# A graph network on one Trainium2 core: fourteen tails of the first layer run as a software pipeline between VectorE and ScalarE

## The chip, the core and the metric

The kernel runs on one core of a Trainium2 chip, as one program. The metric is the device time of one launch in microseconds (us), the median of several runs. All five engines take part: TensorE (PE in the profile, with its weight loads as PEld), VectorE (DVE), ScalarE (ACT), GpSimd (POOL) and SyncE (SP, whose queue issues DMAs).

## The reference, cut to what matters

Four graph layers in a row over 12,500 nodes with 64 features and 212,500 edges. Each layer normalizes `x`, clips it at zero, sums something over the edges into their target nodes and adds the result to `x`. The change lies between the first and the second:

```python
edge_index = jnp.stack([src, dst])
h = jnp.maximum(_layernorm(x, axis=-1), 0.0)
x = x + _L0_gnn_ref(h, L0_gnn_W, src, dst)              # sum of h[src] * W over the edges
h = jnp.maximum(_layernorm(x, axis=-1), 0.0)            # what the changed stage computes
x = x + _L1_gnn_ref(h, edge_index, ...)                 # two mean aggregations with dense layers
...
def _layernorm(x, axis=-1, eps=1e-05):
    m = jnp.mean(x, axis=axis, keepdims=True)
    v = jnp.var(x, axis=axis, keepdims=True)
    return (x - m) / jnp.sqrt(v + eps)
```

## The kernel before, in words

**Layout.** Nodes lie in 98 tiles of 128 (`T` = 98, one node per partition); seven tiles are a batch (`B7` = 7), so there are 14 batches (`NBAT`) of 128 x 448 numbers. `xs` holds x in float32. The sum over the edges is a matrix product with a table of edge counts: `cells` in DRAM holds for each pair of nodes how many edges join them, as bytes, SyncE loads it in chunks of 224 KB, VectorE and ScalarE turn the bytes into bfloat16 by turns (lines 616 and 1400), and TensorE multiplies (line 1650). The other operand is a table `tab` of h, split into three bfloat16 terms (high, middle, low) that add up to the float32 value.

**The first product** (layer 0, `p` = 0) runs beside other work of the kernel. Counts too large for a byte are made up for by a short list: GpSimd adds its sums to `extra` in DRAM, and what it holds is known only at the end of the product. So after the last tile's sums are read out (lines 652 and 653) and the last plain tail (`tail0`, line 755) is done, the loop `for m in range(NBAT): late0(m)` (line 810) runs the 14 late tails, one batch after the other. Nothing of the second product can start before its last table row is made.

**One late tail**, `late0(m)`, is 12 instructions of VectorE and one of ScalarE, in strict order. Line 761 adds the list's counts to `has`, line 762 the list's rows to `xs`. `norm` computes the sum over the features (line 631, to `mean7`), the centred rows (632, `cen`), their squares (633, `sq`) and the sum of the squares (634, `var7`); ScalarE takes the root (1394, `sd7`); VectorE inverts it (637, `rs7`), then scales and clips (638, `hrow`). `split` makes the table's three terms: the high term is a cast (642), the rest a subtraction (643), the middle term a cast (644), the low term a subtraction (645). Then ScalarE's queue issues the DMA of the batch's table rows to `trow` in DRAM (`keep_rows`, line 1403).

**What sets the order.** Each engine's order is that of the text. Every instruction of VectorE here goes through `link`, which raises the semaphore `s_prep` and makes the next instruction wait for it:

```python
def link(ins):
    steps[0] += 1
    ins.then_inc(s_prep, 1)
    dve.wait_ge(s_prep, steps[0])
    return steps[0]
```

On SyncE's queue `load_ext(0, m)` (line 1218) loads the list's rows of batch m into one of two buffers, 227.5 KB each; from the third on it waits until `late0(m - 2)` has read its buffer. After the last of them SyncE issues a load of 832 KB (line 1281) and the first nine chunks of `cells` for the second product, whose ring has nine places. GpSimd waits for all the rows of `trow` and then gathers from it (`list_get`, line 1080).

## Time and profile before

| | |
|---|---|
| median of 3 runs | 6922.79 us (6919.97 to 6924.64) |
| the profiled execution | 6921.18 us, of which the span from the first to the last instruction is 6919.3 us |
| DVE busy | 4606.4 us (67%) |
| ACT busy | 3720.1 us (54%) |
| PE busy | 5262.2 us (76%) |
| late tails (lines 761 to 645, 14 times) | from 2591.62 to 2694.47 us of the span |

The span counts from the first instruction. "Busy" is the time in which an engine has an instruction in hand; the durations of two neighbours on one engine can overlap. "Idle before" a group is the time its engine stood still just ahead of its instructions, with what ended it behind the arrow.

### The profile page before, as it was taken

Reading aid. Unit: us, or ns where it says so; the run is one execution under the profiler, and the core shown is the slowest. Engines: PE = TensorE matmul, PEld = TensorE weight load, DVE = VectorE, ACT = ScalarE, POOL = GpSimd, SP = SyncE. Lnnn points to the kernel's source line nnn. Section 1 sums busy time; section 2 is a strip of 40 time slices with the busy share of each in tenths; the row PEclk is TensorE's granted clock in tenths of the full one; section 3 lists DMA queues with packets and bytes.
Section 4 is the critical chain, followed back from the end, with each engine's and each line's share of the span. In section 5 each row is a group of like instructions: output and inputs, shape, how many; then the busy total and the mean of one; then the engine's idle time right before and its main releaser. Section 6 shows DMA issues by size and latency. Waiting matters only on the chain.

```text
span 6919.3 us, 127730 instructions
## 1 busy us (share of the span) xinstructions
PE 5262.2 (76%) x47666; PEld 4799.9 (69%) x47667; DVE 4606.4 (67%) x6014; ACT 3720.1 (54%) x2906; POOL 3433.8 (50%) x3412
## 2 busy tenths in 40 slices
PE   0057478888888753999999999855888888788886
PEld 0023267777777653999999999855777777677776
DVE  9757567777777658788877888733555555555554
ACT  0100167666666543788777777600555454454565
POOL 0457777777777750000000000077777777777730
PEclk9988789999999886999999999977999999999998
DMA  9999977666666545666666666533777677676785
GB/s 344 351 273 297 335 234 215 209 214 210 212 214 215 175 117 141 181 195 194 191 189 186 195 196 197 161 80 90 158 151 159 153 156 154 140 155 148 157 143 110
DMA packets 1628347, 1313.89 MB, mean 190 GB/s; under 512 B 911250, under 2 KB 1528211, under 8 KB 1627311
## 3 DMA queue, kind: packets, MB, share of 16 engines
q1 hardware_dynamic: 840725, 948.43, 46.1%
q10 hardware_dynamic: 674448, 299.80, 18.4%
q0 software_dynamic: 112592, 57.76, 5.1%
q8 instruction: 382, 6.26, 0.4%
q14 instruction: 200, 1.64, 0.1%
HBM read 833.34 MB, written 311.54 MB: 165 GB/s over the span
## 4 chain that ended last, share of the span: by engine, by line
PE 40%; DVE 7%; ACT 5%; issue 4%; DMA 3%; POOL 3%; DVEq 1%; SPq 0%; ACTq 0%; POOLq 0%
PE pair L1650 22%; PE pair L1769 8%; PE wide L1793 7%; ACT u L1542 3%; POOL u L1151 3%; ACT batch L1542 1%; PE wide L1832 1%; DVE u L918 1%; DMA extra<-hi_b,tsel 1%; DMA u<-zrows,stage 1%; DVEq L415 1%; DVE batch L983 1%; DMA u<-cells 1%; PE flip L1750 0%; DVE u L616 0%
## 5 line engine op out<-in xcount | busy, mean ns | idle before, releaser
L1650 PE MATMUL pair<-tab,u 128*128 128x192 bf16 (+1 forms) x29106 | 2579.5, 249 | 184.9 <-ACT u L1400 179.7
L1650 PEld LDWEIGHTS pair<-tab,u 128*128 128x128 bf16 x29106 | 2503.9, 99 | 213.3 <-ACT u L1400 183.3
L1400 ACT ACTIVATE u<-u 128x1792 bf16<-128x1792 uint8 (+1 forms) x1360 | 2269.6, 1703 | 608.4 <-PE pair L1650 347.4
L1151 POOL DMA_INDIRECT u<-zrows,stage x1664 | 1613.7, 970 | 1318.2 <-DMA zrows<-batch 782.6
L616 DVE TENSOR_REDUCE u<-u 128x1792 bf16<-128x1792 uint8 (+1 forms) x838 | 1675.1, 2021 | 662.9 <-PE pair L1650 508.4
L1116 POOL DMA_INDIRECT cells<-val,idx x1664 | 1727.9, 1038 | 755.2 <-issue 741.7
L1769 PE MATMUL pair<-u 128*128 x4880 | 939.3, 350 | 405.7 <-DVE u L918 388.9
L1769 PEld LDWEIGHTS pair<-u 128*128 128x128 f32 x4880 | 855.8, 204 | 481.6 <-issue 480.3
L1542 ACT ACTIVATE u<-u 128x1792 bf16<-128x1792 uint8 x317 | 524.7, 1684 | 320.8 <-PE wide L1793 313.1
L1609 PE MATMUL wide<-u,wbd 128*128 128x512 f32 (+1 forms) x1120 | 508.9, 588 | 179.4 <-DMA u<-in_ea 108.2
L1632 PE MATMUL flip<-ident,u 128*128 128x128 f32 x840 | 264.7, 329 | 382.9 <-DVE u L752 370.4
L1793 PE MATMUL wide<-u 128*128 128x193 bf16 x5544 | 521.4, 246 | 36.2 <-ACT u L1542 29.8
L1609 PEld LDWEIGHTS wide<-u,wbd 128*128 128x128 f32 x1120 | 235.6, 232 | 407.0 <-issue 314.8
L1793 PEld LDWEIGHTS wide<-u 128*128 128x128 bf16 x5544 | 464.8, 97 | 76.3 <-issue 72.7
L1080 POOL DMA_INDIRECT hi_b<-trow,gsel x24 | 22.8, 952 | 962.3 <-DMA trow<-tab 955.9
L1632 PEld LDWEIGHTS flip<-ident,u 128*128 128x128 f32 x840 | 188.9, 225 | 421.7 <-DVE u L752 403.4
L918 DVE TENSOR_TENSOR u<-wide,idx 128x512 f32<-128x512 f32 x610 | 394.0, 685 | 42.5 <-PE pair L1769 36.6
L1421 ACT ACTIVATE u<-flip 128x512 f32<-128x512 f32 x420 | 247.1, 589 | 303.8 <-PE flip L1633 301.9
L901 DVE TENSOR_TENSOR u<-u (+1 forms) x208 | 144.0, 692 | 367.8 <-SPq L1309 266.6
L733 DVE TENSOR_TENSOR_SCAN u<-u,shared,wide 128x768 f32<-128x768 bf16 x140 | 253.3, 1809 | 198.7 <-issue 113.6
L947 DVE TENSOR_TENSOR nhas<-nhas,wide 128x1 f32<-128x1 f32 x588 | 91.5, 156 | 418.2 <-PE wide L1793 414.0
L725 DVE TENSOR_TENSOR_SCAN u<-u,wide 128x768 f32<-128x768 bf16 x140 | 253.9, 1814 | 163.2 <-DMA u<-gate_d 104.5
(270 smaller groups left out, 4337.4 us busy)
## 6 DMA issues: line engine op xcount, KB each, us to landing
u<-cells SPq DMA_DIRECT2D x2100, 224.0 KB, 3.1
cells<-zt SPq DMA_DIRECT2D x100, 1568.0 KB, 15.7
u<-in_ea SPq DMA_DIRECT2D x280, 384.0 KB
ex_d<-u ACTq DMA_DIRECT2D x280, 384.0 KB, 4.2
u<-ex_d SPq DMA_DIRECT2D x208, 512.0 KB
u<-gate_d SPq DMA_DIRECT2D x280, 96.1 KB
u<-gate_d ACTq DMA_DIRECT2D x280, 96.0 KB
cells<-val,idx POOLq DMA_INDIRECT x1664
```

What stands on the lines that cost most here:

```text
L616: return V.tensor_reduce(to, of.unsqueeze(3), AX.X, ALU.max)
L725: V.tensor_tensor_scan(f_pm[h], f_gate[st % 4], eh[h], f_pm[1 - h][:, SB - 1:SB], ALU.add, ALU.max).then_inc(f_scan, 1)
L918: V.tensor_tensor(ohf[not first][:, k:k + CH // 2, :], base, dcol[:, ds(g * CH + k, CH // 2)].unsqueeze(2).to_broadcast([P, CH // 2, P]), ...
L1116: pool.indirect_dma_start(out=spots, out_offset=bass.IndirectOffsetOnAxis(ap=idx[:, c:c + 1].bitcast(u32), axis=0), in_=val[:, c:c + 1], i ...
L1151: pool.indirect_dma_start(out=ring3[:, slot, k, :], out_offset=None, in_=zrows, in_offset=bass.IndirectOffsetOnAxis(ap=stage[:, st, c:c + ...
L1400: return S.activation(to, of, ACT.Copy)
L1542: S.activation(ring4[n % R4].rearrange("p (b r) -> p b r", b=2), planes(raw4[q % U4]), ACT.Copy).then_inc(e_cast, 1)
L1609: mm = M(eh[h][:, a:b], wbd[:, :], edges[:, a:b], start=True, stop=True)
L1632: TP(flip[w % 2][:, n * 2 * P:n * 2 * P + P], b_pm[st % 3][:, cols], ident[:, :])
L1650: mm = M(acc(p, t // 2 * 2 + b)[:, 0:width], ring[:, q % nr, (b * CK + k) * P:(b * CK + k + 1) * P], table[:, j, 0:width], start=j == 0 an ...
L1769: mm = M(bank[a % 2][:, 0:F3], ohf[not first][:, k, :], exr[:, ds(g % XR, 1), k, :].rearrange("p o c -> p (o c)"), start=first and k == 0, ...
L1793: mm = M(pb[n % 2][:, 0:WC], ring4[n % R4][:, at_k:at_k + P], group[:, k, 0:WC], start=k == 0, stop=k == UT - 1)
```

## The change

The 14 late tails are no longer done one after the other. A loop of 18 steps (`NBAT + 4`) takes, in each step i, one part of each of up to five batches: the sum and the mean and the centred rows of batch i, the variance of batch i - 1, the scale and h of batch i - 2, the rest after the high term of batch i - 3, and the low term of batch i - 4. VectorE's instructions raise `s_prep` as before, but wait only for what they read or overwrite (`step` in place of `link`). Three of VectorE's instructions of a batch go to ScalarE: the squares, the high term and the middle term of the table. Four semaphores carry ScalarE's answers. The centred rows have three buffers, h and its rest two each, variance and root two each, all of it in the tile `batch` or in tiles that are free in this stage. VectorE's wait for `s_gate` in front of its forward scans is gone.

```diff
+        block7 = [batch[:, a * B7 * F:(a + 1) * B7 * F].rearrange("p (t c) -> p t c", t=B7) for a in range(8)]
+        n_cen, n_sqr, n_h, n_low = block7[0:3], block7[3], block7[4:6], block7[6:8]
...
+        n_var, n_sd = [(a[:, :], vtmp[:, b:b + B7]) for a, b in ((var7, 0), (sd7, 8))]
...
+        n_sq, n_root, n_hi, n_mid = sem("n_sq"), sem("n_root"), sem("n_hi"), sem("n_mid")
...
-            def late0(m):
+            def step(ins):
+                steps[0] += 1
+                ins.then_inc(s_prep, 1)
+                return steps[0]
+
+            def late_sum(m):
                 ext = lists_c[5][m % 2]
                 dve.wait_ge(s_ext[m % 2], ext_due(0, m))
+                marks["late", m] = step(V.tensor_tensor(rows7(xs, m), rows7(xs, m), ext[:, :, 0:F], ALU.add))
                 col = has[:, m * B7:(m + 1) * B7].unsqueeze(2)
-                link(V.tensor_tensor(col, col, ext[:, :, F:XW], ALU.add))
-                marks["ext", 0, m] = link(V.tensor_tensor(rows7(xs, m), rows7(xs, m), ext[:, :, 0:F], ALU.add))
-                norm(rows7(xs, m), hrow[:, :, :])
-                marks["tab", 1, m] = split(hrow[:, :, :], tab[1], m)
-
-            dve.wait_ge(s_gate, 64)
+                marks["ext", 0, m] = step(V.tensor_tensor(col, col, ext[:, :, F:XW], ALU.add))
+
+            def late_var(m):
+                dve.wait_ge(n_sq, m + 1)
+                marks["lvar", m] = step(V.tensor_reduce(n_var[m % 2], n_sqr, AX.X, ALU.add))
+
+            def late_mean(m):
+                dve.wait_ge(s_prep, max(marks["late", m], marks["lcen", m - 1] if m else 0))
+                marks["lmean", m] = step(V.tensor_reduce(mean7[:, :], rows7(xs, m), AX.X, ALU.add))
+
+            def late_scale(m):
+                dve.wait_ge(n_root, m + 1)
+                if m:
+                    dve.wait_ge(s_prep, marks["lh", m - 1])
+                marks["lrs", m] = step(V.reciprocal(rs7[:, :], n_sd[m % 2]))
+
+            def late_rest(m):
+                dve.wait_ge(n_hi, m + 1)
+                if m >= 2:
+                    dve.wait_ge(s_prep, marks["tab", 1, m - 2])
+                marks["lrest", m] = step(V.tensor_tensor(n_low[m % 2], n_h[m % 2], rows7(tab[1], m), ALU.subtract))
+
+            def late_centre(m):
+                dve.wait_ge(s_prep, max(marks["lmean", m], marks["lh", m - 3] if m >= 3 else 0))
+                marks["lcen", m] = step(V.scalar_tensor_tensor(n_cen[m % 3], each(mean7[:, :]), -1.0 / F, rows7(xs, m), ALU.mult, ALU.add))
+
+            def late_h(m):
+                dve.wait_ge(s_prep, max(marks["lrs", m], marks["lrest", m - 2] if m >= 2 else 0))
+                marks["lh", m] = step(V.scalar_tensor_tensor(n_h[m % 2], n_cen[m % 3], 0.0, each(rs7[:, :]), ALU.max, ALU.mult))
+
+            def late_low(m):
+                dve.wait_ge(n_mid, m + 1)
+                marks["tab", 1, m] = step(V.tensor_tensor(rows7(tab[1], m, 2 * F, F3), n_low[m % 2], rows7(tab[1], m, F, 2 * F), ALU.subtract))
+
+            def late_all():
+                for i in range(NBAT + 4):
+                    for part, m in ((late_sum, i), (late_var, i - 1), (late_mean, i), (late_scale, i - 2), (late_rest, i - 3),
+                                    (late_centre, i), (late_h, i - 2), (late_low, i - 4)):
+                        if 0 <= m < NBAT:
+                            part(m)
+                dve.wait_ge(s_prep, steps[0])
...
-            for m in range(NBAT):
-                late0(m)
+            late_all()
...
-            for m in range(NBAT):
-                root()
+            def late_root(m):
+                act.wait_ge(s_prep, marks["lvar", m])
+                S.activation(n_sd[m % 2], n_var[m % 2], ACT.Sqrt, bias=epsc[:, :], scale=1.0 / F).then_inc(n_root, 1)
+
+            def late_mid(m):
+                act.wait_ge(s_prep, marks["lrest", m])
+                S.activation(tab[1][:, m * B7:(m + 1) * B7, F:2 * F], n_low[m % 2], ACT.Copy).then_inc(n_mid, 1)
+
+            def late_square(m):
+                act.wait_ge(s_prep, marks["lcen", m])
+                S.activation(n_sqr, n_cen[m % 3], ACT.Square).then_inc(n_sq, 1)
+
+            def late_high(m):
+                act.wait_ge(s_prep, marks["lh", m])
+                S.activation(tab[1][:, m * B7:(m + 1) * B7, 0:F], n_h[m % 2], ACT.Copy).then_inc(n_hi, 1)
+
+            def late_keep(m):
                 act.wait_ge(s_prep, marks["tab", 1, m])
                 keep_rows(tab[1], m)
+
+            for i in range(NBAT + 4):
+                for part, m in ((late_root, i - 1), (late_mid, i - 3), (late_square, i), (late_high, i - 2), (late_keep, i - 4)):
+                    if 0 <= m < NBAT:
+                        part(m)
```

VectorE before, one batch of the late tails (`hi_b` holds the list's rows, `batch` the working tiles; in brackets the semaphores that an instruction waits for):

```order
L761 TENSOR_TENSOR has<-has,hi_b 128x7 [waits s_ext1,s_prep]
L762 TENSOR_TENSOR xs<-xs,hi_b 128x448 [waits s_prep]
L631 TENSOR_REDUCE mean<-xs 128x7 [waits s_prep]
L632 SCALAR_TENSOR_TENSOR batch<-mean,xs 128x448 [waits s_prep]
L633 TENSOR_TENSOR batch<-batch 128x448 [waits s_prep]
L634 TENSOR_REDUCE var<-batch 128x7 [waits s_prep]
L637 RECIPROCAL rs<-sd 128x7 [waits s_root]
L638 SCALAR_TENSOR_TENSOR batch<-batch,rs 128x448 [waits s_prep]
L642 CAST tab<-batch 128x7x64 [waits s_prep]
L643 TENSOR_TENSOR batch<-batch,tab 128x448 [waits s_prep]
L644 CAST tab<-batch 128x7x64 [waits s_prep]
L645 TENSOR_TENSOR tab<-batch,tab 128x7x64 [waits s_prep]
```

VectorE with the change, one step in the middle (`part_1` is the second buffer of the variance and the root):

```order
L769 TENSOR_TENSOR xs<-xs,hi_b 128x448 [waits s_ext1]
L771 TENSOR_TENSOR has<-has,hi_b 128x7
L775 TENSOR_REDUCE var<-batch 128x7 [waits n_sq]
L779 TENSOR_REDUCE mean<-xs 128x7 [waits s_prep]
L785 RECIPROCAL rs<-part_1 128x7 [waits s_prep,n_root]
L791 TENSOR_TENSOR batch<-batch,tab 128x448 [waits s_prep,n_hi]
L795 SCALAR_TENSOR_TENSOR batch<-mean,xs 128x448 [waits s_prep]
L799 SCALAR_TENSOR_TENSOR batch<-batch,rs 128x448 [waits s_prep]
L803 TENSOR_TENSOR tab<-batch,tab 128x7x64 [waits n_mid]
```

Twelve instructions have become nine, those of lines 633, 642 and 644 are gone from this engine, and neighbours belong to different batches.

ScalarE with the change, where the late tails begin and one later step (before, there were a root and a DMA per batch):

```order
L1504 ACTIVATE batch<-batch 128x448 [waits s_prep]
L1496 ACT_TABLE_LOAD
L1496 ACTIVATE sd<-var,epsc 128x7 [waits s_prep]
...
L1496 ACTIVATE sd<-var,epsc 128x7 [waits s_prep]
L1500 ACTIVATE tab<-batch 128x7x64 [waits s_prep]
L1504 ACTIVATE batch<-batch 128x448 [waits s_prep]
L1508 ACTIVATE tab<-batch 128x7x64 [waits s_prep]
L1448 DMA trow<-tab 128x7x194 [waits s_prep]
```

Squares (1504), middle terms (1500) and high terms (1508) are new here; the program loads ScalarE's function table once in this stage, ahead of the first root, as it did before.

## Rows read from the trace of the kernel before

**Rows 1.** Windows: busy us of each engine, TensorE's granted clock, DMA share, GB/s.

```profile
core 0: us, PE busy (x) PEld busy (x) DVE busy (x) ACT busy (x) POOL busy (x), PEclk, DMA share, GB/s
2591.60:2694.50 102.90, 0.00 (x0) 0.00 (x0) 92.47 (x169) 4.20 (x14) 0.00 (x0) 0.52 0.44 100
3000.00:3100.00 100.00, 100.00 (x1160) 97.97 (x1158) 82.59 (x61) 79.85 (x58) 0.00 (x0) 1.00 0.65 189
```

**Rows 2.** Waits between 2585 and 2800 us, longest first.

```profile
engine line waited for: us in total, times, longest us
POOL hi_b L1080 <- DMA trow<-tab: 119.6, 1, 119.6
...
PE pair L1650 <- ACT u L1400: 107.4, 2, 107.0
ACT sd L1394 <- DVE var L634: 99.1, 14, 7.5
```

**Rows 3.** Groups of instructions of DVE between 2591.5 and 2694.4 us.

```profile
L762 DVE TENSOR_TENSOR xs<-xs,hi_b 128x448 f32<-128x448 f32 x14 | 8.8, 626 | 0.5
...
L634 DVE TENSOR_REDUCE var<-batch 128x7 f32<-128x448 f32 x14 | 8.7, 620 | 0.5
L637 DVE RECIPROCAL rs<-sd 128x7 f32<-128x7 f32 x14 | 2.8, 201 | 5.1 <-ACT sd L1394 5.1
L761 DVE TENSOR_TENSOR has<-has,hi_b 128x7 f32<-128x7 f32 x14 | 2.4, 171 | 0.5
```

**Rows 4.** Timeline of the end of the stage: start us, us, instruction.

```profile
2687.12 0.17 DVE L761 TENSOR_TENSOR has<-has,hi_b 128x7 f32<-128x7 f32 x1
2687.32 0.63 DVE L762 TENSOR_TENSOR xs<-xs,hi_b 128x448 f32<-128x448 f32 x1
...
2694.47 0.21 DVE L812 TENSOR_SCALAR dinv<-has 128x98 f32<-128x98 f32 x1
...
2696.71 8.69 PE L1650 MATMUL pair<-tab,u 128*128 128x192 bf16 x70 [106.95 <-ACT u L1400]
```

**Rows 5.** Timelines of DVE elsewhere: the sort at 60 us, the backward stage at 1508 us.

```profile
59.27 1.23 DVE L459 TENSOR_TENSOR u<-u 128x1024 f32<-128x1024 f32 x1
60.41 1.22 DVE L460 TENSOR_TENSOR u<-u 128x1024 f32<-128x1024 f32 x1
61.66 1.23 DVE L459 TENSOR_TENSOR u<-u 128x1024 f32<-128x1024 f32 x1
...
1508.18 0.95 DVE L752 TENSOR_TENSOR u<-wide,u 128x768 f32<-128x768 f32 x1
1509.05 1.81 DVE L741 TENSOR_TENSOR_SCAN u<-u,carry 128x768 f32<-128x768 bf16 x1
```

**Rows 6.** Groups of ACT by shape: copies and squares ahead of the first product, the root.

```profile
L1363 ACT ACTIVATE tab<-u 128x1600 bf16<-128x1600 f32 x4 | 6.2, 1540 | 9.4 <-DVE u L577 6.3 <-DVE u L583 3.1
L1363 ACT ACTIVATE tab<-u 128x1536 bf16<-128x1536 f32 x4 | 5.9, 1486 | 9.4 <-DVE u L577 4.8 <-DVE u L583 4.6
L1353 ACT ACTIVATE u<-tab 128x1536 f32<-128x1536 f32 x2 | 3.0, 1483 | 4.5 <-DVE tab L564 4.5
L1394 ACT ACTIVATE sd<-var,epsc 128x7 f32<-128x7 f32 x28 | 8.4, 300 | 165.9 <-DVE var L634 165.9
```

**Rows 7.** Timeline there: a square on ACT beside a reduction on DVE.

```profile
278.43 1.76 DVE L564 SCALAR_TENSOR_TENSOR tab<-has,xs 128x1536 f32<-128x1536 f32 x1
...
280.23 1.48 ACT L1353 ACTIVATE u<-tab 128x1536 f32<-128x1536 f32 x1 [2.04 <-DVE tab L564]
280.23 1.75 DVE L570 TENSOR_REDUCE dinv<-u 128x24 f32<-128x1536 f32 x1
```

**Rows 8.** DMA between 2607 and 2651 us: queues (share of 16 engines), issues, median us to landing.

```profile
q1 hardware_dynamic: 5472, 1.40, 21.0%
q10 hardware_dynamic: 5472, 2.09, 19.8%
...
trow<-tab ACTq DMA_DIRECT2D x6, 339.5 KB, 4.5
hi_b<-extra SPq DMA_DIRECT2D x6, 227.5 KB, 4.0
```

**Rows 9.** DMA between 2673 and 2690 us: q1 is SyncE's queue.

```profile
q1 hardware_dynamic: 2352, 3.15, 58.0%
...
u<-cells SPq DMA_DIRECT2D x9, 224.0 KB, 7.2
...
hi_b<-extra SPq DMA_DIRECT2D x1, 227.5 KB, 5.8
```

**Rows 10.** Windows around the start of the second product; columns as in rows 1.

```profile
2690.00:2695.00 5.00, 0.00 (x0) 0.00 (x0) 4.39 (x9) 0.34 (x2) 0.00 (x0) 0.50 0.00 0
...
2715.00:2720.00 5.00, 0.00 (x0) 0.00 (x0) 1.60 (x1) 1.70 (x1) 0.00 (x0) 0.78 0.87 169
```

## The prediction

> **What bounds the kernel now.** I read the windows first, to find what the changed stage is made of. In its 102.9 us TensorE and GpSimd do nothing, ScalarE is busy for 4.2 us, VectorE for 92.5 us [rows 1]. The waits say who is held up: TensorE stands still for 107.0 us until ScalarE converts the next product's first chunk, GpSimd for 119.6 us until the table rows have landed, ScalarE for 99.1 us on the variance, a batch at a time [rows 2]. So the stage is one chain on VectorE, and each us taken from it is a us of the kernel, as long as what follows starts from it and from nothing else. It does: the second product's conversions stand behind the last table row on both engines [rows 4], and from there TensorE is busy 100 us in 100 [rows 1]. The groups give the price of an instruction [rows 3], the timelines how close two of them can stand [rows 4, 5].
>
> **One batch before.** Ten instructions of 620 to 626 ns, one of 201, one of 171 [rows 3], each followed by a gap of 0.5 / 14 = 0.035 us, since it waits for the one ahead; only the reciprocal has 5.1 / 14 = 0.36 ahead of it, ScalarE's root. The stage runs from 2591.62 (the time table of the text ahead) to 2694.47 us, where the instruction behind it starts [rows 4]: 102.85 us, 7.35 a batch.
>
> **What is taken away.** Squares and the two casts leave VectorE. Seven large instructions are left, and the two small ones; the wait for the root is covered, since the reciprocal now comes a step later.
>
> **How close the rest can stand.** This is the term that decides the size. Where an instruction waits for the one just ahead, the next starts 0.03 us after its end: 60.41 + 1.22 against 61.66. Where it doesn't, it starts 0.085 before its end: 59.27 + 1.23 = 60.50 against 60.41 [rows 5]. The same at 1508.18, where 0.95 us of work are followed after 0.87, although the follower waits for three other semaphores, long raised [rows 5]. In the new order no instruction of a full step waits for its immediate neighbour: the mean waits for the sum three places ahead, the centred rows for the mean three places ahead, h for the reciprocal three places ahead. So I take 0.623 - 0.085 = 0.538 us for each of seven large ones, 0.171 - 0.085 = 0.09 for the counts and 0.201 - 0.085 = 0.12 for the reciprocal: 3.77 + 0.21 = 3.97 us a batch. The two ends of this term: with the gap of 0.035 behind each, it is 7 x 0.658 + 0.21 + 0.24 = 5.05 us; with the overlap, 3.97. I take the second, because the rows with the same kind of neighbourhood show it.
>
> The Trainium skill speaks against it: "VectorE: DVE Perf Modes", section "The DRAIN you can't avoid", says that instructions without semaphores between them take the same time as with them, so that only their number counts. By that, the stage would lose 14 x 2.3 = 32 us and not 46, by my estimate. The same section adds that an instruction that is not held starts earlier; this trace agrees with that addition, at 60.41 us [rows 5].
>
> **ScalarE's side, hidden.** A copy to the table of 1600 numbers takes 1540 ns, of 1536 numbers 1486 [rows 6]: 0.84 ns a number and 0.19 us fixed, so 0.57 us for 448. The square of 1536 takes 1483 ns, the same within 3 ns, so 0.57 too. With the root of 0.30 and the issue of a DMA of 0.37 that is 3 x 0.57 + 0.30 + 0.37 = 2.4 us of a step of 3.97. Squares beside a reduction on VectorE take no longer than alone, and an answer from one engine to the other takes 0.04 us (278.43 + 1.76 = 280.19, ScalarE starts at 280.23) [rows 7]. The tightest wait in a full step: centred rows start 2.35 us into it and end at 2.98, the squares end at 3.6, and the variance wants them at 3.97 + 0.63 = 4.6. That is 1.0 us of slack; the high term has 1.6, the others over 4. If ScalarE took twice as long for these three, 3.4 + 0.67 = 4.1 us a step, it would be level with VectorE and cost 0.1 us a step.
>
> **Both ends of the pipeline.** In the first two steps the mean and the squares are waited for (0.2 us in all, with the first step's instructions back to back). In the last four steps few instructions are left between a question and its answer: the rest of batch 12 waits 0.06, that of batch 13 0.2, its low term 0.2. Together 0.7 us, and 0.1 for the last end. The function table is loaded behind the first squares, 1.3 us that end before the first root is asked for at 3.2 us plus what the reciprocal has to spare; it costs nothing.
> The stage: 14 x 3.97 + 0.8 = 56.4 us. **Gain: 102.85 - 56.4 = 46.5 us.**
>
> **The DMAs that this makes crowd.** Each batch loads list rows and writes table rows, 21.0% + 19.8% of the 16 DMA engines over 44 us with six of each [rows 8]: 1.5 + 1.45 = 3.0 us a batch, which fits in 3.97. A list load lands after 4.0 us [rows 8], 5.8 at most [rows 9], and has two steps less the sum, 7.3 us. At the end SyncE loads 832 KB and nine chunks. Before, they were issued at 2673.9, right behind the list's last load, and all was down by 2690 [rows 10], using 58.0% of 17 us = 9.9 us of the engines [rows 9]; 21 us were there. Now, by the step at which batch 11 has read its buffer, 17 us are there, and with six table writes at 1.45 the demand is 9.9 + 8.7 = 18.6 us. The first chunks arrive in time, the last late by 1 or 2 us, and the seven conversions of the start take the ring's chunks over some 7 us. But DMA is short right behind that (0.87 busy with TensorE idle [rows 10]), so the debt may show. Bounds: 0, and 2.6 us (9.9 us at half the engines are 19.8 of 17.2) with two table writes, together 5.5. I take **1 us**, nearer to 0, since the chunks are wanted in order and early ones are early.
>
> **The rest costs nothing.** The order of the two additions in `late_sum` changes what a list load waits for by one small instruction. The wait for `s_gate` on VectorE was met long before: ScalarE waits for it too and VectorE waits for ScalarE's squares ahead of that place. TensorE's clock was granted 0.52 in this stage, the lower level (1.2 GHz), after standing idle [rows 1], and 56 us of idleness will bring it there too. GpSimd, with no work of its own, starts its gathers when the rows land, so it moves with the stage. What stands behind, moves forward unchanged.
>
> **Sum.** 46.5 - 1 = 45.5 us. The profiled execution took 6921.2 and would take 6875.7; the median of the runs, 1.6 us above it, 6877.3.
>
> **Rivals.**
> *No overlap.* Each instruction costs its gap, whatever it waits for, as in rows 3: 14 x 5.05 + 0.7 = 71.4 us, a gain of 31.5, so 6891.3. For it: instructions here raise a semaphore each and are short. Against it: those of the sort raise one each too, and overlap [rows 5]. This is also what the skill's rule above gives.
> *DMA debt.* The chunks of the second product are late by the 5.5 us above: 6922.8 - 46.5 + 5.5 = 6881.8. For it: DMA bounds the product's first 25 us already. Against it: 5 us without any traffic before the start [rows 10].
> *The gain is caught up later.* Something after the stage is due at its own time, and the end moves by less than 13.8 us. For it: nothing that I find; GpSimd and TensorE both wait through the stage [rows 2].
> *Slower: the list's round trip sets the pace.* Two buffers hold the list rows, so two batches cannot take less than landing, sum and counts and issue: at 4.0 us it is 4.0 + 0.7 + 0.1 = 4.8 us for two batches, 2.4 each, hidden; at 7.2 us, the longest median among these loads [rows 9], 4.0 each, level with VectorE. At 15.8 us it would be 8.3 us each, the stage 117 us, 14 us longer than now: 6936.8. With 3.0 us of DMA work in each 3.97 the landings may grow, but hardly fourfold.
>
> **How the numbers follow.** A change of about 0.2%, 13.8 us, can just be told from none. Forecast (6873.5 to 6879.5): 0.71. No overlap: 0.12. DMA debt: 0.12. Caught up later: 0.03. Round trip: 0.02. Faster by over 0.2% in the first three: 0.95; the same 0.03, slower 0.02. The range takes in the first three: from 6873.5 (no debt, 6876.3, and an overlap of 0.1 in place of 0.085, 9 x 0.015 x 14 = 1.9 us, and a little noise) to 6891.5.
>
> **What would show it.** In the profile after: the seven large instructions of VectorE each 14 times at about 0.62 us, starts 0.54 apart in the middle of the stage; if they are 0.66 apart, the first rival holds. The stage about 56 us, a step 4.0. No wait of VectorE on ScalarE of more than 0.3 us, and only in the last steps. Squares and copies on ScalarE at 0.57. TensorE's wait for the first chunk down from 107 to about 61 us. List loads landing in 4 to 6 us. If VectorE waits in the sums (line 769) for the list's DMA, the round trip has come up; if TensorE or the conversions wait longer for chunks in the 25 us after the stage than before, the debt has.

## The result and the profile after

The changed kernel takes 6871.1 us (median of 5 runs, 6856.89 to 6884.75), the kernel before 6920.84 (5 runs, 6916.78 to 6924.64). The ratio is 0.9929 with a 95% interval from 0.9913 to 0.9944, which is 39 to 60 us: faster, as forecast, but by 49.7 us by the medians and not by 45.5, and 2.4 us below the lower end of the range. The five runs of one and the same changed kernel lie up to 28 us apart.

The profiled executions took 6921.18 and 6868.52 us; their spans, 6919.3 and 6866.6, differ by 52.7. Four stretches add up to it, but for rounding:

| stretch | before | after | difference |
|---|---|---|---|
| start to the first late sum | 2591.6 | 2586.3 | -5.3 |
| the late stage | 102.9 | 55.5 | -47.3 |
| from its end to the second product's first tail (line 826, now 871) | 129.4 | 136.2 | +6.8 |
| from there to the end | 4095.5 | 4088.7 | -6.8 |

Only the second row is where the change was expected to pay. What the others are is asked below.

Timeline of the changed kernel, one step of the pipeline (start us, us, engine, line, instruction; in brackets the idle time before it). It answers to [rows 3, 4]:

```profile
2620.20 0.63 DVE L769 TENSOR_TENSOR xs<-xs,hi_b 128x448 f32<-128x448 f32 x1
...
2620.74 0.18 DVE L771 TENSOR_TENSOR has<-has,hi_b 128x7 f32<-128x7 f32 x1
2620.82 0.63 DVE L775 TENSOR_REDUCE part<-batch 128x7 f32<-128x448 f32 x1
...
2621.34 0.63 DVE L779 TENSOR_REDUCE mean<-xs 128x7 f32<-128x448 f32 x1
...
2621.87 0.21 DVE L785 RECIPROCAL rs<-sd 128x7 f32<-128x7 f32 x1
2621.98 0.59 DVE L791 TENSOR_TENSOR batch<-batch,tab 128x448 f32<-128x448 f32 x1
2622.47 0.63 DVE L795 SCALAR_TENSOR_TENSOR batch<-mean,xs 128x448 f32<-128x448 f32 x1
2622.61 0.58 ACT L1500 ACTIVATE tab<-batch 128x448 bf16<-128x448 f32 x1 [0.82 <-DVE batch L791]
2623.01 0.64 DVE L799 SCALAR_TENSOR_TENSOR batch<-batch,rs 128x448 f32<-128x448 f32 x1
2623.14 0.58 ACT L1504 ACTIVATE batch<-batch 128x448 f32<-128x448 f32 x1
2623.54 0.64 DVE L803 TENSOR_TENSOR tab<-batch,tab 128x448 bf16<-128x448 f32 x1
2623.68 0.58 ACT L1508 ACTIVATE tab<-batch 128x448 bf16<-128x448 f32 x1
2624.07 0.64 DVE L769 TENSOR_TENSOR xs<-xs,hi_b 128x448 f32<-128x448 f32 x1
```

The large instructions still take 0.63 us each, but start 0.53 apart; sum to sum it is 3.87 us, where a batch took 7.35. VectorE has no gap, and ScalarE's three jobs take 0.58 each and lie wholly beside it.

The waits of the changed kernel between 2586 and 2755 us (us in total, times, longest) answer to [rows 2]:

```profile
POOL hi_b L1125 <- DMA trow<-tab: 82.8, 1, 82.8
...
PE pair L1715 <- ACT u L1445: 67.4, 3, 62.8
...
DVE u L620 <- DMA u<-cells: 13.2, 4, 6.9
...
ACT u L1445 <- DMA u<-cells: 9.8, 3, 5.0
...
ACT u L1445 <- issue: 4.4, 1, 4.4
```

TensorE waits 62.8 us for its first chunk and not 107.0. That is 44.1 less, not 47.3: 3.2 us are lost behind the stage. The last row shows what holds it up, ScalarE held for 4.4 us by its own queue. In the timeline, the last table rows' DMA issue there takes 2.43 us, where one took 0.37 in mid-stage, and TensorE starts 5.4 us behind the stage's end and not 2.2:

```profile
2642.97 2.43 ACTq L1448 DMA_DIRECT2D trow<-tab  x1
...
2645.53 3.29 ACT L1445 ACTIVATE u<-u 128x1792 bf16<-128x1792 uint8 x2 [4.38 <-issue]
...
2647.28 0.98 PE L1715 MATMUL pair<-tab,u 128*128 128x192 bf16 x5 [62.81 <-ACT u L1445]
```

The rows on `u<-cells` say that chunks came late too. In the 35 us behind the stage, VectorE waits 11.7 us in all for chunks and ScalarE 4.8, together 16.5; behind the stage of the kernel before it was 6.9 and 5.6, together 12.5.

The windows (columns as in [rows 1]) show the crowd of DMAs behind it, and that [rows 10] has no idle 5 us any more:

```profile
2600.00:2625.00 25.00, 0.00 (x0) 0.00 (x0) 25.00 (x59) 12.68 (x26) 0.00 (x0) 0.50 0.68 140
...
2635.00:2640.00 5.00, 0.00 (x0) 0.00 (x0) 4.89 (x12) 3.41 (x7) 0.00 (x0) 0.50 1.13 347
2640.00:2645.00 5.00, 0.00 (x0) 0.00 (x0) 4.72 (x8) 0.58 (x1) 0.00 (x0) 0.50 1.32 156
2645.00:2650.00 5.00, 2.72 (x18) 2.59 (x19) 5.00 (x4) 4.47 (x3) 0.00 (x0) 0.50 1.29 124
```

### The profile page after: what moved, and what is told of

Read it like the earlier page. It is cut to its first block, busy times and chain, and to the rows that moved or that the text cites. A ratio compares the mean times of both kernels' runs of the same rounds, so it can differ in the third digit from the quotient of the medians.

```text
span 6866.6 us, 127741 instructions
## 1 busy us (share of the span) xinstructions
PE 5256.4 (77%) x47666; PEld 4797.5 (70%) x47667; DVE 4569.1 (67%) x5972; ACT 3742.9 (55%) x2948; POOL 3433.3 (50%) x3412
## 4 chain that ended last, share of the span: by engine, by line
PE 40%; DVE 6%; ACT 5%; issue 4%; DMA 3%; POOL 3%; DVEq 1%; SPq 0%; ACTq 0%; POOLq 0%
PE pair L1715 22%; PE pair L1834 8%; PE wide L1858 7%; ACT u L1607 3%; POOL u L1196 3%; ACT batch L1607 2%; DMA u<-zrows,stage 1%; DMA extra<-hi_b,tsel 1%; DVE u L963 1%; PE wide L1897 1%; DMA u<-cells 1%; DVEq L419 1%; DVE batch L1028 1%; PE flip L1815 0%; DVE u L620 0%
## 5 line engine op out<-in xcount | busy, mean ns | idle before, releaser
L1715 PE MATMUL pair<-tab,u 128*128 128x192 bf16 (+1 forms) x29106 | 2581.4, 250 | 146.1 <-ACT u L1445 141.9
L1161 POOL DMA_INDIRECT cells<-val,idx x1664 | 1727.5, 1038 | 754.7 <-issue 493.1
```

The source lines that it names most:

```text
L1161: pool.indirect_dma_start(out=spots, out_offset=bass.IndirectOffsetOnAxis(ap=idx[:, c:c + 1].bitcast(u32), axis=0), in_=val[:, c:c + 1], i ...
L1715: mm = M(acc(p, t // 2 * 2 + b)[:, 0:width], ring[:, q % nr, (b * CK + k) * P:(b * CK + k + 1) * P], table[:, j, 0:width], start=j == 0 an ...
```

## The experiments

Three questions: what makes the stage shorter (the pipeline, ScalarE's help, or both); what the crowd of DMAs costs; and whether the other stretches are the change's doing. Each kernel was timed beside the kernel before on the same chip, so gains are compared as ratios.

**The changed kernel again** (`e1_again`, no edit).

> The changed kernel once more, to part what the change does from what the runs scatter. In its first profile the late stage was 47.3 us shorter, but it also began 5.3 us earlier, and the time from the second product to the end was some 6.9 us shorter; between them 7 us were lost at the start of the second product. Theory A (chance): begin of the stage and the third layer scatter from run to run, the stage and the loss at its end do not. Then the stage is again 55.5 us (within 0.5), the first product's matmul again 5 to 6 us behind its end, the begin anywhere within 5 us of 2589, and the median 6871 to 6881. Theory B (the change also does something ahead of the stage): the begin is again within 1 us of 2586.3, and the median 6868 to 6872.

Measured: 6866.45 us against 6913.57, ratio 0.9931 (0.9918 to 0.9945). The stage takes 55.9 us, but begins at 2602.5 us, 16 us later than in the first profile, and 11 us later than before the change. So the earlier begin is no part of the change, and theory B is refuted. Theory A is right in that the begin scatters, but it missed three of its own marks: the begin lies well outside "within 5 us of 2589", the median is below 6871, and the loss behind the stage did scatter. From the stage's end to the first tail it takes 129.2 us, as before the change, and not 136.2, although TensorE again starts 5.2 us behind the stage's end. (The stage's 0.4 us more are a wait of VectorE for the last middle term, held up on ScalarE behind a DMA issue of 1.11 us.)

**The wait for the gates put back** (`e2_gate_back`).

```diff
+            dve.wait_ge(s_gate, 64)
             link(V.memset(f_pm[1], 0.0))
```

> The changed kernel with VectorE's wait for s_gate put back. Theory A: the semaphore is long raised there, so nothing moves: within 4 us of the changed kernel in the same round, begin of the late stage within its scatter. Theory B: the wait held VectorE back or sets the phase of the forward scans; then the begin goes back to 2591 or later and the whole is 4 to 6 us slower than the changed kernel.

Measured: 6862.55 us, ratio 0.9931 (0.9917 to 0.9944), the stage 55.5 us, its begin at 2585.6. The wait costs nothing that these runs can tell.

**No overlap** (`e3_linked`): the same instructions, each waiting for the one ahead.

```diff
             def step(ins):
                 steps[0] += 1
                 ins.then_inc(s_prep, 1)
+                dve.wait_ge(s_prep, steps[0])
                 return steps[0]
```

> The changed kernel with every VectorE instruction of the late stage waiting for the one ahead of it, same instructions in the same order. Theory of the overlap (my forecast): neighbours stand 0.12 us further apart, nine of them in 14 batches: 14 x 9 x 0.12 = 15 us, stage 55.5 + 15 = 70.5 us. The whole then is 10 to 15 us slower than the changed kernel, the lower end if the DMA debt at the end of the stage (7 us) shrinks with the slower pace. Rival (only the number of instructions counts): stage within 1 us of 55.5, whole unchanged.

Measured: 6885.16 us, ratio 0.9963 (0.9949 to 0.9976); the stage 71.0 us, 15.5 more. The whole is 18.7 us slower than `e1_again` of the same round, where 10 to 15 were expected. Its timeline:

```profile
2621.03 0.62 DVE L776 TENSOR_REDUCE var<-batch 128x7 f32<-128x448 f32 x1
2621.68 0.62 DVE L780 TENSOR_REDUCE mean<-xs 128x7 f32<-128x448 f32 x1
2622.34 0.20 DVE L786 RECIPROCAL rs<-part 128x7 f32<-128x7 f32 x1
2622.57 0.62 DVE L792 TENSOR_TENSOR batch<-batch,tab 128x448 f32<-128x448 f32 x1
2623.23 0.63 DVE L796 SCALAR_TENSOR_TENSOR batch<-mean,xs 128x448 f32<-128x448 f32 x1
```

Starts stand 0.65 or 0.66 apart behind a large instruction, where the changed kernel has 0.53. A wait for the neighbour costs 0.12 us an instruction, 126 times, with the same instructions in the same order. The overlap theory holds, and the statement of the Trainium skill that a semaphore after each chained instruction costs nothing extra ("VectorE: DVE Perf Modes", section "The DRAIN you can't avoid") does not hold here.

**The pipeline alone** (`e4_all_dve`): squares, high and middle terms stay on VectorE as three more parts of a step.

```diff
+            def late_sqr(m):
+                dve.wait_ge(s_prep, max(marks["lcen", m], marks["lvar", m - 1] if m else 0))
+                marks["lsq", m] = step(V.tensor_tensor(n_sqr, n_cen[m % 3], n_cen[m % 3], ALU.mult))
...
-                                    (late_centre, i), (late_h, i - 2), (late_low, i - 4)):
+                                    (late_centre, i), (late_h, i - 2), (late_md, i - 3), (late_sqr, i), (late_hi, i - 2),
+                                    (late_low, i - 4)):
```

> The pipeline over the batches without ScalarE's help: squares, high and middle terms stay on VectorE, ten large instructions and two small ones a batch, none waiting for its neighbour. Forecast by the overlap theory: 10 x 0.54 + 0.21 = 5.6 us a batch, stage 14 x 5.6 + 0.5 = 79 us, that is 24 us less than before and 23.5 more than the changed kernel. Rival (the three instructions' relief is all there is, pipelining gives nothing but the covered root): 10 x 0.658 + 0.44 = 7.0 us a batch, stage 99 us, 4 us less than before. The DMA debt should be gone at this pace, so the whole is 6895 to 6900 by the first and 6915 to 6919 by the second.

Measured: 6885.99 us, ratio 0.9962 (0.9948 to 0.9976); the stage 77.5 us, 25.3 less than before. About 5 of these are the wait for the root, now covered, and 20 the overlap (12 instructions, 14 batches, 0.12 us each). The stage is 1.5 us shorter than expected, but the whole is 9 us below the 6895 to 6900 of the forecast: that sum began from another round's 6921, and in this round the kernel before takes 6913.57. Here two of the three instructions that the changed kernel gives to ScalarE, 0.53 us apart:

```profile
2622.22 0.60 DVE L813 CAST tab<-batch 128x448 bf16<-128x448 f32 x1
2622.75 0.60 DVE L805 TENSOR_TENSOR batch<-batch 128x448 f32<-128x448 f32 x1
```

**ScalarE's help alone** (`e9_offload_serial`): the same parts, one batch after the other.

```diff
-                for i in range(NBAT + 4):
...
+                for m in range(NBAT):
+                    for part in (late_sum, late_mean, late_centre, late_var, late_scale, late_h, late_rest, late_low):
+                        part(m)
...
+            for m in range(NBAT):
+                for part in (late_square, late_root, late_high, late_mid, late_keep):
+                    part(m)
```

> ScalarE's three jobs without the pipeline: the changed kernel's parts, but one batch after the other, so that every answer is waited for. Forecast by the chain: on VectorE the sums 0.63 and 0.09, mean 0.66, centred rows 0.65, the square on ScalarE 0.04 + 0.58 + 0.04, variance 0.62, root 0.38, reciprocal 0.20, h 0.66, high term 0.66, rest 0.59, middle term 0.66, low term 0.62: some 7.2 us a batch, stage 100 to 102 us, within 3 us of before. The whole then is within 3 us of the kernel before in the same round. Rival (relieving VectorE is what pays): three instructions fewer, 14 x 3 x 0.66 = 28 us less than before, stage 75.

Measured: 6904.76 us against 6910.6, ratio 0.9991 (0.9982 to 1.0); the stage 97.0 us, 5.9 less than before and 3 less than my chain gave. The whole, too, gained more than the 3 us expected, 5.8 by the medians, with an interval that ends at no change. VectorE now stands still for each answer:

```profile
2620.95 0.58 ACT L1506 ACTIVATE tab<-batch 128x448 bf16<-128x448 f32 x1 [0.93 <-DVE batch L799]
2621.56 0.62 DVE L791 TENSOR_TENSOR batch<-batch,tab 128x448 f32<-128x448 f32 x1 [0.64 <-ACT tab L1506]
2622.22 0.58 ACT L1498 ACTIVATE tab<-batch 128x448 bf16<-128x448 f32 x1 [0.69 <-DVE batch L791]
2622.83 0.63 DVE L803 TENSOR_TENSOR tab<-batch,tab 128x448 bf16<-128x448 f32 x1 [0.65 <-ACT tab L1498]
2623.37 0.62 DVE L769 TENSOR_TENSOR xs<-xs,hi_b 128x448 f32<-128x448 f32 x1
...
2623.90 0.17 DVE L771 TENSOR_TENSOR has<-has,hi_b 128x7 f32<-128x7 f32 x1
2624.02 0.62 DVE L779 TENSOR_REDUCE mean<-xs 128x7 f32<-128x448 f32 x1
```

A hand-over costs 0.65 us, as much as the instruction that was handed over. What makes the stage shorter is mostly something else. This kernel has `step` and not `link`, so the sum, the counts and the mean don't wait for the instruction just ahead of them. From the low term to the mean it takes 1.19 us (2622.83 to 2624.02), where the kernel before takes 1.52:

```profile
2620.35 0.62 DVE L645 TENSOR_TENSOR tab<-batch,tab 128x448 bf16<-128x448 f32 x1
2621.01 0.17 DVE L761 TENSOR_TENSOR has<-has,hi_b 128x7 f32<-128x7 f32 x1
2621.21 0.62 DVE L762 TENSOR_TENSOR xs<-xs,hi_b 128x448 f32<-128x448 f32 x1
2621.87 0.62 DVE L631 TENSOR_REDUCE mean<-xs 128x7 f32<-128x448 f32 x1
```

That is 0.33 us a batch, between 4 and 5 of the 5.9 us in 13 or 14 batches. The four kernels side by side:

| late stage, us | VectorE does all | ScalarE helps |
|---|---|---|
| one batch after the other | 102.9 | 97.0 |
| pipeline over batches | 77.5 | 55.5 |

ScalarE's help is worth 22.0 us in the pipeline. In the order of before it is worth 5.9 us at most, and only 1 to 2 by the estimate above, since the upper row differs by the three waits as well; no run has ScalarE's help with all of `link`'s waits.

**The kernel before again** (`e5_before_again`, no edit).

> The kernel before once more, to see how far it scatters by stage. Theory A (what lies ahead of and behind the stage scatters by itself): the late stage again 102.85 us within 0.3; its begin anywhere between 2581 and 2602 us; from the stage's end to the second product's first tail 120 to 130 us; the third layer's loop 2124 to 2135. Theory B (the changed kernel is also faster elsewhere): begin 2591 and the loop 2128 again, both within 1 us.

Measured: 6942.64 us (11 runs) against 6939.3 of the same kernel (15 runs), ratio 1.0004 (0.9995 to 1.0013). The stage is 102.8 us again and begins at 2606.5, 15 us later than in the first profile; 129.8 us pass from its end to the first tail. So the stage and what follows it hold still in these two profiles, and the begin does not: 2602 was the latest that theory A allowed. The begin goes with the group of GpSimd's scatters into `cells`, which the first product waits for. Here the group (busy us, mean ns) of three kernels, the one before again, then `e7_keep_late` and `e8_both_late` (below), whose stages begin at 2606.5, 2581.4 and 2609.0 us:

```profile
L1116 POOL DMA_INDIRECT cells<-val,idx x1664 | 1749.0, 1051 | 754.0 <-issue 491.6 <-SPq L1194 247.1 <-DMA cells<-val,idx 14.3
```

```profile
L1161 POOL DMA_INDIRECT cells<-val,idx x1664 | 1723.5, 1036 | 755.5 <-issue 494.1 <-SPq L1239 246.5 <-DMA cells<-val,idx 14.0
```

```profile
L1161 POOL DMA_INDIRECT cells<-val,idx x1664 | 1751.9, 1053 | 754.9 <-issue 494.6 <-SPq L1239 246.6 <-DMA cells<-val,idx 13.7
```

Over the 14 profiles of this study, 1723.5 to 1731.3 us of busy time go with a begin from 2581.4 to 2591.6, and 1745 to 1752 us with 2601.8 to 2609.0; the one between, 1734.8 us, with 2591.1. Within the first group the begin still moves by 10 us at nearly the same busy time (2591.6 with 1727.9 us, 2586.3 with 1727.5), so the scatters are not all of it. That they are the cause is argued from this and not tried, nor is what makes the same 1664 instructions take 1% longer.

**The large load moved away** (`e6_dcol_late`).

```diff
-            sp.dma_start(dcol_i, dst_cols).then_inc(s_dcol, 16)
             for p in (1, 2):
+                if p == 2:
+                    sp.dma_start(dcol_i, dst_cols).then_inc(s_dcol, 16)
```

> The changed kernel with the load of 832 KB moved from ahead of the second product's chunks to ahead of the third's. Theory of the DMA debt: the DMA engines are full from 2630 us on (share over 1) and the first chunks stand behind this load, so from the stage's end to the first tail it takes 3 to 6 us less than the 129 to 136 of the changed kernel, and the whole is 2 to 6 us faster. Rival: the time there is set by the short list's serial adds, which follow the gathers, and these the table rows; then at most 1 us.

**Meant: the last table rows' issues behind the first conversions** (`e7_keep_late`). The kernel that ran has only this in addition, a function that nothing calls:

```diff
+            LAST = 4
+
+            def late_keep_early(m):
+                if m < NBAT - LAST:
+                    late_keep(m)
```

> The changed kernel with the DMA issues of the last four batches' table rows moved behind ScalarE's first conversions of the second product. Theory: the three issues that end the stage hold ScalarE for 4.4 us and TensorE for 3.2 of them; then TensorE starts 2.2 us behind the stage's end in place of 5.2, and the first tail comes 3 us sooner. The rows land later, by 10 to 20 us, which costs nothing as the list's sums are wanted only some 60 us in. Rival: the rows' traffic then meets the chunk loads, and the 3 us are lost again before the first tail: no change.

**Meant: both** (`e8_both_late`). Of the two moves, the kernel that ran has only that of the large load, and again the function that nothing calls.

> Both moves together. If the two costs are separate: from the stage's end to the first tail 6 to 8 us less than the changed kernel, the whole 5 to 8 us faster, some 6860. Rival, both pay for one and the same shortage of DMA: no more than the better of the two alone.

Measured, all against 6939.3: 6885.72, 6887.47 and 6885.33 us, ratios 0.9923, 0.9924 and 0.9923 (the widest interval 0.9909 to 0.9938). Two of the three are not what they were meant to be. `e7_keep_late` is the changed kernel once more; its trace has the last table rows' issues where they were, the last at 2638.07 us, ahead of the first conversion at 2640.24. `e8_both_late` is `e6_dcol_late` once more. So the theories on moving the table rows' issues, alone or together with the load, remain untested.

What the three do give is the large load's move with the changed kernel beside it in the same round. The whole differs by 2 us, less than these intervals can tell. From the stage's end to the first tail it takes 129.2 and 128.5 us with the load moved (`e6`, `e8`). The changed kernel has 129.2, 127.4, 130.9 (`e1`, `e11`, `e7`) and once 136.2, and `e2_gate_back` 129.2; the kernel before has 129.4 and 129.8. TensorE starts 3.6 and 4.7 us behind the stage's end with the load moved, and 5.0 to 5.4 without. So the forecast of 3 to 6 us less to the first tail failed, and the rival fits. The traces show why. In each of the 14 profiles GpSimd's nine serial adds into `extra` stand ahead of the first tail. They begin 77.0 us behind the stage's end before the change and 79.9 in the first profile after it, and the chain from their end to the first tail is (start us, us, what):

```profile
2761.51 3.20 DMA extra<-vboth,vsel
...
2767.17 5.18 DMA u<-cells
...
2772.37 2.02 DVE u L620
```

Of the 6.8 us by which the first profile was late there, 2.9 had built up before the adds and 3.0 came in the adds (39.8 us from the first to the last where the kernel before takes 36.8). `e3_linked` and `e4_all_dve`, whose stages are slower, start TensorE after 2.2 and 2.3 us and reach the first tail after 123.4 and 125.1. But `e9_offload_serial` starts it after 2.2 too and needs 131.7, and `e12_pool_apart` (below), with the shortest stage, starts it after 2.2 and needs 127.3. What decides between 123 and 132 us, these runs don't tell.

**The low term on GpSimd** (`e10_pool_low`).

```diff
...
+            for m in range(NBAT):
+                pool.wait_ge(n_mid, m + 1)
+                pool.tensor_tensor(tab[1][:, m * B7:(m + 1) * B7, 2 * F:F3], n_low[m % 2],
+                                   tab[1][:, m * B7:(m + 1) * B7, F:2 * F], ALU.subtract).then_inc(n_lo, 1)
...
```

> The changed kernel with the low term (line 803) made by GpSimd, which waits through the stage. It takes one large instruction of 0.54 us off VectorE's step of 3.92: 3.38 us a batch, stage 48 us, 7 us less, if GpSimd makes 448 numbers in under 3.3 us. ScalarE needs 2.4 us a step and is covered. Rival: GpSimd is slower than 3.4 us for it, or hinders VectorE; then the stage is set by it, 14 times its time. DMA: list and table rows need 2.9 us of the 16 engines a batch, 0.86 of a step of 3.38; if the DMA is what ends the wait for the second product, less than the 7 us is seen in the whole.

Measured: 6863.48 us against 6910.6, ratio 0.9928 (0.9914 to 0.9942), no different from the changed kernel. The stage is 59.7 us, 4.2 longer, with one instruction less. GpSimd is quick enough at 1.25 us; the rival's second half came true. Timeline:

```profile
2610.65 0.61 DVE L799 SCALAR_TENSOR_TENSOR batch<-batch,rs 128x448 f32<-128x448 f32 x1
...
2610.88 1.25 POOL L1183 TENSOR_TENSOR tab<-batch,tab 128x448 bf16<-128x448 f32 x1 [2.90 <-ACT tab L1506]
2611.18 1.43 DVE L769 TENSOR_TENSOR xs<-xs,hi_b 128x448 f32<-128x448 f32 x1
...
2612.53 0.15 DVE L771 TENSOR_TENSOR has<-has,hi_b 128x7 f32<-128x7 f32 x1
```

VectorE's sum takes 1.43 us instead of 0.62, and ends 0.48 us after GpSimd (2610.88 + 1.25 = 2612.13). It looks as if it could read only from then on.

**The same, with the two kept apart** (`e12_pool_apart`): behind h come the two reductions. The order of ScalarE's jobs is changed to match.

```diff
-                for i in range(NBAT + 4):
-                    for part, m in ((late_sum, i), (late_var, i - 1), (late_mean, i), (late_scale, i - 2), (late_rest, i - 3),
-                                    (late_centre, i), (late_h, i - 2), (late_low, i - 4)):
+                for i in range(NBAT + 5):
+                    for part, m in ((late_sum, i), (late_scale, i - 3), (late_rest, i - 4), (late_centre, i - 1),
+                                    (late_h, i - 3), (late_var, i - 2), (late_mean, i), (late_low, i - 4)):
...
```

> The kernel with the low term on GpSimd, its VectorE steps in another order: sum, counts, reciprocal, rest, centred rows, h, variance, mean. In the run before, VectorE's sum (two inputs in SBUF) took 1.43 us and ended 0.48 us after GpSimd's subtraction had ended; all others kept their 0.61. Theory (VectorE's instructions with two SBUF inputs and GpSimd's subtraction exclude each other): with the two reductions, one input each, behind h, nothing meets GpSimd's 1.25 us; the sum is back at 0.6 us, a step is 3.4 us, the stage 14 x 3.4 + 2 = 49 to 51 us, and the whole 4 to 7 us less than the changed kernel. Rival (any VectorE instruction waits for GpSimd): then the variance or the mean takes 1.4 us, and the stage stays at 58 to 61 us.

Measured: 6852.86 us (5 runs) against 6916.3 (8 runs), ratio 0.9911 (0.9897 to 0.9925). The stage is 52.2 us, a step 3.34:

```profile
2609.74 0.62 DVE L799 SCALAR_TENSOR_TENSOR batch<-batch,rs 128x448 f32<-128x448 f32 x1
2609.97 1.24 POOL L1183 TENSOR_TENSOR tab<-batch,tab 128x448 bf16<-128x448 f32 x1 [2.09 <-ACT tab L1506]
2610.27 0.61 DVE L775 TENSOR_REDUCE part<-batch 128x7 f32<-128x448 f32 x1
...
2610.80 0.61 DVE L779 TENSOR_REDUCE mean<-xs 128x7 f32<-128x448 f32 x1
...
2611.33 0.62 DVE L769 TENSOR_TENSOR xs<-xs,hi_b 128x448 f32<-128x448 f32 x1
```

The reductions, one input each, run at full speed beside GpSimd, and the sum is back at 0.62, behind GpSimd's end. The Trainium skill states the rule ("SBUF — State Buffer", section "Summary: rules for kernel authors", on VectorE and GpSimd running together: with two inputs in SBUF on VectorE and a GpSimd operation that reads SBUF, the second waits for the first); this pair of runs agrees. It holds the other way round too: GpSimd's subtraction takes 1.24 to 1.25 us wherever it starts while h, with two inputs, is still running, and 1.00 or 1.01 in the three last batches of either run, where it starts alone or beside the end of a small instruction or a reduction.

The stage missed its forecast of 49 to 51 by 1.2 us, all at its two ends: 2.0 us in which VectorE waits for GpSimd's last subtraction, 1.1 us of waiting for the last high term, 0.7 for the last two roots, and 0.5 for a list load in the third step, while the pipeline fills:

```profile
2586.27 0.63 DVE L769 TENSOR_TENSOR xs<-xs,hi_b 128x448 f32<-128x448 f32 x1 [0.49 <-DMA hi_b<-extra]
...
2634.90 0.21 DVE L859 TENSOR_SCALAR dinv<-has 128x98 f32<-128x98 f32 x1 [2.04 <-POOL tab L1183]
```

By its stage this is the fastest version of the study, 3.3 us below the changed kernel's; by the ratios, 0.9911 against 0.9919 to 0.9931, the intervals still overlap, so that the whole is faster is not shown.

**The changed kernel a third time** (`e11_again`, no edit).

> The changed kernel a third time, beside the two above. Stage 55.5 us; from its end to the second product's first tail 129 us as in two of three profiles (136 in the first); begin of the stage between 2581 and 2608, later where GpSimd's 1664 scatters took longer (1723.5 us of busy time went with 2580.7, 1751.9 with 2608.4); gain over the kernel before, by medians of the same round, 42 to 52 us.

Measured: 6856.72 us against 6910.6, ratio 0.9919 (0.9906 to 0.9933); the stage 55.5 us, its begin 2591.1, 127.4 us to the first tail. The gain by medians, 53.9 us, is just above what was expected.

## Why the prediction was right or wrong

**The chain on VectorE bounds the stage, and what follows moves with it:** right. The stage lost 47.3 us, and three measurements of the changed kernel gave 49.7, 47.1 and 53.9 us by medians, the unintended fourth (`e7`) 51.8. All four intervals hold 47.3 us, a ratio of 0.9932. One step of the reading was too simple: TensorE is busy 100 us in 100 at 3000 us, but not "from there", since it stands still again 20 us behind the stage [rows 10], and the first tail waits for GpSimd's adds. Those too start from the stage's end, so the gain is passed on all the same.

**How close instructions can stand:** right, and the step that carried the forecast. It was put at 3.97 us a batch, and is 3.87 or 3.88. What was off is the starts that follow a small instruction or the rest: 0.49 us behind the rest (line 791 to 795) where I took 0.54, 0.08 and 0.11 where I took 0.09 and 0.12, and 0.53 behind the others for 0.538. That is 1.4 us less in 14 batches; the two ends of the pipeline cost 1.3 us and not 0.8. Together the stage is 55.5 and not 56.4, a mis-sized term of 0.9 us. `e3_linked` confirms its other end, 71.0 against the 71.4 written for the rival without overlap.

**ScalarE's side hidden:** right; 0.58 us a job against 0.57, no wait of VectorE in a full step, and the table load at no cost.

**The DMA debt, taken at 1 us:** as a size not refuted, as a mechanism incomplete. The late chunks came: in the 35 us behind the stage VectorE and ScalarE together wait 16.5 to 18.1 us for chunks in the five profiles of kernels with this stage (the changed kernel four times, and `e2`), and 12.5 and 11.5 in the two of the kernel before. What the sum did not have is ScalarE's own queue, holding it for up to 4.4 us at the stage's end, 3 us for TensorE. Neither is seen at the first tail, where four of the five profiles show 127.4 to 130.9 us against 129.4 and 129.8 before. The first profile's 6.8 us did not come back in any other.

**What stands ahead and behind costs nothing and moves unchanged:** here the forecast missed. The step that failed is this term, put at nothing ("The rest costs nothing", "What stands behind, moves forward unchanged"), together with the "little noise" at the lower end of the range. In the first pair of profiles the time ahead of the stage is 5.3 us shorter and that behind the first tail 6.8 us shorter, with 6.8 us lost between. The 5.3 us are scatter and not the change's doing; of the other two the same is likely, but not shown. The begin of the stage lies anywhere from 2581.4 to 2609.0 us in 14 profiles, at 2591.6 and 2606.5 in the two of the kernel before, and the kernel before has medians from 6910.6 to 6942.6 us in six measurements. The "little noise" rested on three runs within 5 us of each other.

How the miss adds up: 6877.3 was forecast and 6871.1 measured, 6.2 us less. Of this, 2.0 us are the starting value (6922.8 from three runs, 6920.8 from five), 0.9 the stage, 1 us the debt if it is nothing, and 2.3 us are left, which no run assigns to a cause. As far as these runs show, that the median fell just outside the range is chance: the range should have been at least 10 us wider on either side, and the stage itself came out within 1 us.

**Rivals.** No overlap: refuted by the starts 0.53 us apart and by `e3_linked`. DMA debt: late chunks in every profile, but a later first tail in one of five. Caught up later: not seen; the gain stays to the end. Round trip: absent in the changed kernel, where list loads landed after 3.9 us in the median and 6.0 at most; in `e12` a list load is waited for once, 0.5 us while the pipeline fills, and never at its full step of 3.34.

**Open.** Seven measurements of kernels with a stage of 55.5 to 55.9 us (four of the changed kernel, three variants) gave ratios from 0.9919 to 0.9931, on average 0.9926, which is 51 us, 3 to 4 more than the stage's. Each interval includes the stage's 0.9932. From the first tail to the end, the kernel before takes 4095.5 and 4095.8 us, the changed kernel 4088.7, 4088.0, 4090.0 and 4091.1. But the two runs of one program with the load moved take 4098.5 and 4087.8, so this stretch scatters by 10 us by itself. Whether something beyond the stage became faster, these runs don't settle.

## What to carry to other kernels

Where one engine works a chain in which each instruction waits for its neighbour, interleave independent batches before anything else: it takes 0.12 us off every instruction here and covers every answer from another engine, and only then is handing work to a second engine worth much (22.0 us with it; without it 5.9 at most, mostly from waits dropped on the way). When GpSimd helps beside VectorE, place VectorE's reductions, the single-input instructions tried here, where GpSimd reads SBUF. And take the spread for a range from several rounds on more than one chip, not from three runs that agree.

## What the runs showed of the hardware

- VectorE's instructions on 128 x 448 float32 numbers take 0.62 to 0.63 us, but start 0.65 to 0.66 us apart where each waits for the one just ahead and 0.53 where it waits for older ones only (`e3_linked` against the changed kernel).
- GpSimd's subtraction of 128 x 448 numbers and a VectorE instruction with two inputs in SBUF exclude each other: started during the subtraction, VectorE's sum took 1.43 us in place of 0.62, while reductions beside it kept 0.61; started during VectorE's h, the subtraction took 1.24 us in place of 1.00 (`e10`, `e12`).
- A DMA issue on ScalarE's queue, 0.37 us otherwise, took 1.82 and 2.43 us as the last two of three issues within 3.1 us, while the DMA engines were full (share 1.32), and held ScalarE with it. Full engines alone did not do it: in `e12_pool_apart`, with the same share of 1.32 but issues 2.4 to 2.7 us apart, the last three took 0.91, 0.68 and 0.44. What decides was not tried.
- GpSimd's 1664 indirect scatters took 1723.5 to 1751.9 us in different profiles of the same instructions, 1036 to 1053 ns each, and the late stage, behind them, began at times up to 28 us apart.
